# M and N kept unsplit and split on the chip, feed-forward weights split in their ring

## The chip, the cores and the metric

The kernel runs on one core of one Trainium2 chip. The metric is the device time of one execution in microseconds (us). The five engines are named as the profile names them: PE (TensorE, matrix products; PEld is its weight load), DVE (VectorE), ACT (ScalarE), POOL (GpSimd) and SP (SyncE, which here does nothing but issue DMAs, in the order of its program).

## The reference

Two attention layers in float32 over x of 4 batches x 1024 rows x 512:

```
layer 0: q = x wq + bq, k = ctx wk + bk, v = ctx wv + bv      (16 heads of 64, ctx is 64 rows per batch)
         x = LN(softmax(q k'/8 + 2 fside) v wo + bo + x)
layer 1: x = attn(LN1 x, LN1 x) + x      self-attention, 16 heads of 32; q, k, v and weights rounded to 8 bits
         x = attn(LN2 x, ctx) + x        cross-attention, likewise
         x = ((LN3 x) w1a + b1a) * gelu((LN3 x) w1g + b1g) w2 + b2 + x     feed-forward, 512 -> 2048 -> 512
```

The rounding steps need products of nearly float32 precision. So each float32 operand of such a product is split into a high part (float32 rounded to the PE's fp32r format) and a low part (what is left, value minus high), and one product is three matmuls (`three`): high*high, high*low, low*high.

## The kernel before

**Setup.** Layer 0's score matrix is x (wq k'), and its output is p (v wo). Since ctx has only 64 rows per batch, the kernel first multiplies the weights together: for each batch b a matrix M (512 x 1024: all heads' wq k') and a matrix N (1024 x 512: v wo). They are made in groups of four PSUM banks: `GROUPS` has 8 groups of M (4 for each half) and 8 of N. For each group ACT rounds the banks into a staging buffer `st_hi` (`high_rows_M` L998, `high_rows_N` L1009), DVE subtracts into `st_lo` (L1252), and SP stores both to HBM (`kept`): two DMAs for a group of M (L541), eight for one of N (L553). There are two staging buffers of each kind, so ACT waits before a group until the group two earlier has been stored. The raw weights come in through `raw0/raw1` and are split by ACT (L978) and POOL (L816). The setup ends when SP has waited for all stores (its first DMA after it is that of `crow`, L656).

**Chunks.** x is worked in 8 chunks of 512 rows, two for each batch. For a batch: `cross(n)` for its two chunks (layer 0, then q1, k1, v1 of layer 1), then `self_attention(n)` and `middle(n)` (cross-attention, LN3) for each. In `cross` eight steps i compute scores: half 0 (i 0 to 3) with block M0, half 1 with M1; each goes PE -> DVE (add the bias `fbias`, row maximum, subtract) -> ACT (exp) -> DVE (sum) -> POOL (scale, L860) -> PE (transpose, L1808) -> ACT/DVE (split) -> PE (product with N0 or N1). Scores of all steps share PSUM bank 0, so PE's next scores wait until DVE has read the last. POOL adds `crow` to each `fbias` (L853) before DVE can use it.

**Weight blocks.** M0, N0, M1, N1, q1, k1, v1, o1, q2, o2 are 512 x 512 blocks, each loaded by SP as two DMAs, high and low (`load_block`, L604, L605), into one of three slots. A slot is loaded when the block that was in it has been used.

**Feed-forward.** Its 12 groups of steps (`F_ORDER`) use 24 pieces of weights, loaded (`load_piece`, L616, L617) into a ring of 3 pieces. The steps of chunk n are spread as a guest over the slots of later stages (`feed`): for an even chunk over the self-attention and the middle of the next chunk, for an odd one over the next batch's cross, self-attention and middle, for the last one alone. Plans (`host_quarters`) say how many quarter steps are due in each slot; `steps_due` with a lag in slots says when ACT (lag 2) and POOL (lag 3) do their part.

**Prep.** The blocks o1, q2, o2 and the feed-forward weights (15 pieces of work, list `PREP`) aren't split in the setup but during batch 0, through one buffer: SP loads `prep_raw` (L669), ACT rounds (`prep_high`, L1068), POOL subtracts (`prep_low`, L823), SP stores both parts (`keep_prep`, L676, L682). Four are in cross(0), four in cross(1), seven in self_attention(0). SP waits for a store's source and for the buffer between its other DMAs; behind the last of cross(1) it issues the DMA that turns the queries (`turn_queries`, L738), which self_attention(0) needs.

The order on every engine is fixed by the program: each engine has one list of instructions, and waits in it hold all that stands behind.

## Time and profile before

| | |
|---|---|
| time, median of 3 runs | 3646.42 us (3646.25 to 3647.31) |
| the profiled execution | 3642.84 us, its span 3641.0 us |
| PE busy in the span | 2990.9 us (82%) |
| DVE, ACT, POOL busy | 2200.3, 1625.9, 1329.3 us (60%, 45%, 37%) |
| granted PE clock, mean | 0.895 of full speed |
| DMA | 518.20 MB, mean 142 GB/s |

Busy shares are means over stages that differ much. The span begins with the setup (to 224.75 us), then batch 0 (its two crosses to about 527 us, its self-attentions and middles to about 1107 us), then three batches of about 795 us each. In the page's picture of 40 slices of 91 us PE is busy 4, 4, 3, 7, 5, 5, 5 tenths in the first seven slices and 7 to 9 tenths in all but one of those behind them. In a timeline row the first number is the start and the second the time to the end of the row's last instruction, both in us; "[a <-X]" is how long the engine sat idle before it, and what ended that.

### The profile page before, as it was taken

How to read it: one execution, taken by the hardware profiler on the slowest of the kernel's cores; microseconds unless marked ns; L12 is line 12 of the kernel's file. 1: busy time of each engine (PE TensorE's matmuls, PEld its weight loads, DVE VectorE, ACT ScalarE, POOL GpSimd, SP SyncE). 2: the span in 40 equal slices, each digit the busy share in tenths (PEclk: the TensorE clock that was granted, in tenths of full speed). 3: DMA queues.
4: the chain of work that ended last, by engine and by line, in shares of the span. 5: the costliest groups of instructions: out<-in, count | busy, mean ns of one | idle time of the engine just before them, and what ended most of it. 6: DMA issues, size and time to landing. Idle time of an engine off the chain costs nothing.

```text
span 3641.0 us, 50850 instructions
## 1 busy us (share of the span) xinstructions
PE 2990.9 (82%) x19712; PEld 2172.7 (60%) x19712; DVE 2200.3 (60%) x3575; ACT 1625.9 (45%) x2666; POOL 1329.3 (37%) x1025
## 2 busy tenths in 40 slices
PE   4437555769988988989989988889988898899999
PEld 3336442445667765656667755666767655665777
DVE  2335347858756459668656559678465569578431
ACT  3322125637632237547532248457323258367221
POOL 2141315625433215445432225345241335344221
PEclk8668775579999999989999999989999999999999
DMA  6884634322345431332344521332444421332334
GB/s 199 298 286 154 235 123 168 128 110 82 121 151 219 139 148 47 140 122 82 151 153 170 197 84 71 133 116 82 166 165 165 170 79 67 123 116 82 150 129 171
DMA packets 228975, 518.20 MB, mean 142 GB/s; under 512 B 96769, under 2 KB 113409, under 8 KB 206721
## 3 DMA queue, kind: packets, MB, share of 16 engines
q1 hardware_dynamic: 216320, 513.33, 38.9%
q10 hardware_dynamic: 12416, 1.62, 0.3%
q8 instruction: 158, 2.59, 0.3%
q14 instruction: 81, 0.66, 0.1%
HBM read 428.39 MB, written 82.31 MB: 140 GB/s over the span
## 4 chain that ended last, share of the span: by engine, by line
PE 53%; DVE 22%; ACT 7%; issue 5%; POOL 5%; DMA 5%; SPq 2%; ACTq 1%; POOLq 0%; DVEq 0%
PE psum L1587 16%; PE psum L1588 14%; PE psum L1589 14%; DVE mx L1467 8%; DVE w1T L1486 4%; PE psum L1869 3%; DVE den L1473 2%; PE psum L1857 2%; ACT e L1162 2%; ACT psum L1075 1%; SPq L553 1%; DMA kept<-st_lo 1%; ACT ht_hi L1074 1%; PE psum L1883 1%; DVE gate L1378 1%
## 5 line engine op out<-in xcount | busy, mean ns | idle before, releaser
L881 POOL TENSOR_SCALAR w1b<-e,rec 128x1024 f16<-128x1024 f32 x512 | 573.1, 1119 | 717.9 <-DVE rec L1475 501.1
L1467 DVE TENSOR_REDUCE mx<-psum 128x1 f32<-128x1024 f32 x512 | 621.9, 1215 | 74.8 <-PE psum L1858 74.8
L1162 ACT ACTIVATE e<-psum,nb,scale 128x1024 f32<-128x1024 f32 x512 | 617.5, 1206 | 16.8
L1587 PE MATMUL psum<-h_hi,fw_hi 128*128 128x512 f32 x1024 | 465.8, 455 | 16.4 <-DVE h_lo L1252 9.0
L1588 PE MATMUL psum<-h_lo,fw_hi 128*128 128x512 f32 x1024 | 418.0, 408 | 0.0
L1589 PE MATMUL psum<-h_hi,fw_lo 128*128 128x512 f32 x1024 | 417.5, 408 | 0.0
L1869 PE MATMUL psum<-ident,w1b 128*128 128x128 f16 x4096 | 351.3, 235 | 79.8 <-DVE w1T L1486 76.5
L1869 PEld LDWEIGHTS psum<-ident,w1b 128*128 128x128 f16 x4096 | 260.3, 105 | 248.4 <-issue 212.1
L1486 DVE TENSOR_SCALAR w1T<-psum 128x1024 bf16<-128x1024 f16 x512 | 348.6, 681 | 97.5 <-PE psum L1869 92.3
L1587 PE MATMUL psum<-w_hi,ht_hi 128*128 128x512 f32 x640 | 265.9, 415 | 60.7 <-DVE e L1404 32.5
L1341 DVE TENSOR_TENSOR x<-psum,x 128x512 f32<-128x512 f32 x224 | 152.2, 684 | 260.3 <-PE psum L1589 259.9
L1587 PEld LDWEIGHTS psum<-h_hi,fw_hi 128*128 128x128 f32 x1024 | 200.4, 196 | 136.1 <-issue 101.0
L829 POOL TENSOR_TENSOR rstd<-ve,mhalf 128x1 f32<-128x1 f32 x128 | 87.0, 680 | 515.3 <-DVE ve L1349 515.3
L1156 ACT ACTIVATE nb<-mx,nscale 128x1 f32<-128x1 f32 x512 | 149.9, 293 | 278.0 <-DVE mx L1467 270.1
L1588 PE MATMUL psum<-w_lo,ht_hi 128*128 128x512 f32 x640 | 258.8, 404 | 0.0
L1589 PE MATMUL psum<-w_hi,ht_lo 128*128 128x512 f32 x640 | 257.8, 403 | 0.0
L1587 PE MATMUL psum<-fw_hi,u_hi 128*128 128x512 f32 x512 | 226.4, 442 | 22.0 <-POOL u_lo L890 10.4
L890 POOL TENSOR_TENSOR u_lo<-gate,u_hi 128x512 fp32r<-128x512 f32 x128 | 164.0, 1284 | 213.8 <-ACT u_hi L1096 207.8
L1589 PEld LDWEIGHTS psum<-h_hi,fw_lo 128*128 128x128 f32 x1024 | 202.0, 197 | 47.3
L1858 PE MATMUL psum<-k_odd,q_turned 32*128 32x512 bf16 x512 | 220.1, 431 | 0.0
L1588 PEld LDWEIGHTS psum<-h_lo,fw_hi 128*128 128x128 f32 x1024 | 203.2, 198 | 25.9
L1019 ACT ACTIVATE qt<-psum,rounder,inv 128x512 f32<-128x512 f32 x128 | 99.9, 780 | 254.9 <-PE psum L1589 254.9
(175 smaller groups left out, 5904.1 us busy)
## 6 DMA issues: line engine op xcount, KB each, us to landing
fw_hi<-pieces SPq DMA_DIRECT2D x192, 512.0 KB, 3.3
fw_lo<-pieces SPq DMA_DIRECT2D x192, 512.0 KB, 4.3
w_hi<-kept SPq DMA_DIRECT2D x80, 1024.0 KB, 5.0
w_lo<-kept SPq DMA_DIRECT2D x80, 1024.0 KB, 7.7
fbias<-in_fside_Bx16xSxS SPq DMA_DIRECT2D x64, 256.0 KB, 3.5
prep_raw<-in_L_xattn_ff_w SPq DMA_DIRECT2D x12, 1024.0 KB, 8.0
pieces<-prep_hi SPq DMA_DIRECT2D x24, 512.0 KB, 3.5
pieces<-prep_lo SPq DMA_DIRECT2D x24, 512.0 KB, 5.5
```

Of the source, the lines that this page charges most:

```text
L881: pool.tensor_scalar(w1b[u % NH][:], e1[u % NE][:], rec1[:, u % 8:u % 8 + 1], HALF, ALU.mult, ALU.add).then_inc(w1_ready.sem, 1)
L890: pool.tensor_tensor(u_lo[:, m, :], gate[:, m, :], u_hi[:, m, :].bitcast(F32), ALU.subtract).then_inc(u_lo_done.sem, 1)
L1156: act.activation(nb1[:, s % 4:s % 4 + 1], mx1[:, s % 4:s % 4 + 1], ACT.Copy, scale=nscale[:, 0:1]).then_inc(nb_ready.sem, 1)
L1162: act.activation(e1[s % NE][:], psum[:, i:i + 2, :].rearrange("p i n -> p (i n)"), ACT.Exp, bias=nb1[:, s % 4:s % 4 + 1], scale=scale[:, 0:1],
L1341: return emptied_bank(dve.tensor_tensor(xt, bank(bank_of(key)), xt, ALU.add), key)
L1467: dve.tensor_reduce(mx1[:, s % 4:s % 4 + 1], psum[:, i:i + 2, :].rearrange("p i n -> p (i n)"), AX, ALU.max).then_inc(maxed1.sem, 1)
L1486: emptied_bank(dve.tensor_scalar(w1T[u % 8][:].rearrange("p k q -> p (k q)"), bank(bank_of(key)).bitcast(FP16), -HALF, W_HIGH, ALU.add, AL ...
L1587: pe.matmul(o, s_hi, m_hi, start=first, stop=False)
L1588: pe.matmul(o, s_hi, m_lo, start=False, stop=False)
L1589: return pe.matmul(o, s_lo, m_hi, start=False, stop=last)
L1858: ins = pe.matmul(bank(i + 1), q1_turned[turned, hg, t * P:t * P + P], k1[1][turned, hg, :], start=True, stop=True)
L1869: ins = pe.transpose(bank(bank_of(key)).bitcast(FP16)[:, k * P:k * P + P], w1b[u % NH][:, k * P:k * P + P], ident16[:])
```

## The change

M and N are copied from PSUM once, unsplit, half of the banks by ACT and half by DVE, into one of four staging buffers (`st0` to `st3`, in the room of the four of before), and stored once: one DMA for a group of M, four for one of N, into `mixed`. A block M0, N0, M1 or N1 is loaded by one DMA into `w_mixed` (the room of its low part), rounded by ACT (`block_high`, 128 x 2048) and subtracted by POOL (`block_low`, four instructions of 128 x 512) at fixed places: M0 and N0 of the batch's second chunk between its two crosses, M0 of the next batch at the end of the middle before it, the others inside the loop over i. PE waits for the low parts instead of the DMA.

`PREP` keeps only o1, q2 (cross(0)) and o2 (cross(1)). The feed-forward pieces of chunk 0 are loaded from the kernel's inputs into the ring (`unsplit`, in the room of the low part), rounded by ACT (`piece_high`, 128 x 1024) and subtracted by POOL (`piece_low`) in place, and stored from there (`keep_piece`) for the other seven chunks. A piece's place in the ring is loaded again only after that store. The first three are done in middle(0), the other 21 in the slots of chunk 0's feed, ACT with a lag of 2 slots, POOL 3, SP's store 4 (1 each in a middle).

```diff
-LAG_HIGH, LAG_LOW = 2, 3
+LAG_HIGH, LAG_LOW, LAG_KEEP = 2, 3, 4
 def steps_due(plan, lag, i):
     def ended(i):
-        last = max(j - (lag if j in plan.late else 1) for j in range(i - 3, i + 1))
+        last = max(j - (lag if j in plan.late else 1) for j in range(i - lag, i + 1))
         last = min(last, len(plan.ends) - 1)
         return plan.ends[last] // 4 if last >= 0 else 0
     return range(ended(i - 1), ended(i))
+def pieces_due(plan, lag, i):
+    return [v + F_RING for k in steps_due(plan, lag, i) for v in range(PIECES - F_RING) if PIECE_END[v] == k]
...
+PREP = ["o1", "q2", "o2"]
+PREP_IN = {0: ["o1", "q2"], 1: ["o2"]}
...
-GROUP_DMAS = {"M": 2, "N": 8}
+GROUP_DMAS = {"M": 1, "N": 4}
+STAGED = 4
...
             def store_rows_M(half, j):
-                g = GROUPS.index(("M", half, j))
+                g = GROUPS.index(("M", half, j)) % STAGED
+                wait_emptied(sp, ("M", half, j, 1, 0))
                 wait_emptied(sp, ("M", half, j, 1, 1))
-                for part, st in enumerate((st_hi, st_lo)):
-                    sp.dma_start(kept[B * half:B * half + B, part, :, 512 * j:512 * j + 512].rearrange("b p n -> p b n"),
-                                 st[g % 2][:].bitcast(F32)).then_inc(group_stored[g % 2], 16)
+                sp.dma_start(mixed[B * half:B * half + B, :, 512 * j:512 * j + 512].rearrange("b p n -> p b n"), st[g][:]
+                             ).then_inc(group_stored[g], 16)
             def store_rows_N(m):
-                g = GROUPS.index(("N", m))
+                g = GROUPS.index(("N", m)) % STAGED
+                wait_emptied(sp, ("N", m, 1, 0))
                 wait_emptied(sp, ("N", m, 1, 1))
                 r = 8 + B * (m // 4)
-                for part, st in enumerate((st_hi, st_lo)):
-                    for h in range(2):
-                        for odd in range(2):
-                            dst = kept[r:r + B, part, 64 * h:64 * h + 64, 512 * (m % 4):512 * (m % 4) + 512]
-                            sp.dma_start(dst.rearrange("(g o) p n -> o p g n", o=2)[odd],
-                                         st[g % 2][64 * odd:64 * odd + 64, 2 * h:2 * h + 2, :].bitcast(F32)
-                                         ).then_inc(group_stored[g % 2], 16)
+                for h in range(2):
+                    for odd in range(2):
+                        dst = mixed[r:r + B, 64 * h:64 * h + 64, 512 * (m % 4):512 * (m % 4) + 512]
+                        sp.dma_start(dst.rearrange("(g o) p n -> o p g n", o=2)[odd],
+                                     st[g][64 * odd:64 * odd + 64, 2 * h:2 * h + 2, :]).then_inc(group_stored[g], 16)
...
-                sp.dma_start(flat(w_hi[s]), kept[kept_row(key), 0]).then_inc(w_loaded[s], 16)
-                sp.dma_start(flat(w_lo[s]), kept[kept_row(key), 1]).then_inc(w_loaded[s], 16)
+                if name in MIXED:
+                    sp.dma_start(w_mixed[s][:].rearrange("p k n -> p (k n)"), mixed[mixed_row(key)]).then_inc(w_loaded[s], 16)
+                else:
+                    sp.dma_start(flat(w_hi[s]), kept[KEPT[name], 0]).then_inc(w_loaded[s], 16)
+                    sp.dma_start(flat(w_lo[s]), kept[KEPT[name], 1]).then_inc(w_loaded[s], 16)
...
+                if n == 0:
+                    if v >= F_RING:
+                        wait_piece_kept(sp, v - F_RING)
+                    w, row, col = SOURCE[F_ORDER[v // 2]]
+                    if F_ORDER[v // 2][0] == "d":
+                        src = a[w][row + 256 * (v % 2):row + 256 * (v % 2) + 256, :]
+                    else:
+                        src = a[w][:, col + 256 * (v % 2):col + 256 * (v % 2) + 256]
+                    n_cols = src.shape[1]
+                    sp.dma_start(unsplit[r][:].rearrange("p (k n) -> p k n", n=n_cols),
+                                 src.rearrange("(k p) n -> p k n", p=P)).then_inc(raw_piece_loaded[r].sem, 16)
+                    return
                 if r == F_RING:
                     wait_filled(sp, ("a1", n, HG - 1))
-                wait_prep_kept(sp, F_ORDER[v // 2])
+                if n == 1 and v >= PIECES - F_RING:
+                    wait_piece_kept(sp, v)
                 sp.dma_start(fw_hi[r][:].bitcast(F32), pieces[v, 0]).then_inc(f_loaded[r], 16)
                 sp.dma_start(fw_lo[r][:].bitcast(F32), pieces[v, 1]).then_inc(f_loaded[r], 16)
+            def keep_piece(v):
+                r = PIECE_SLOT[0, v]
+                sp.wait_ge(piece_lo_done.sem, piece_lo_done.at(v))
+                sp.dma_start(pieces[v, 0], fw_hi[r][:].bitcast(F32)).then_inc(piece_kept[r].sem, 16)
+                sp.dma_start(pieces[v, 1], fw_lo[r][:].bitcast(F32)).then_inc(piece_kept[r].sem, 16)
             def feed(n, plan, i):
+                if n == 0:
+                    for v in pieces_due(plan, LAG_KEEP, i):
+                        keep_piece(v)
...
-                    load_prep(PREP[4 * n])
+                    load_prep(PREP_IN[n][0])
                 for i in range(3, 7):
                     load_fbias(n, i)
                 load_block((n, "N1"))
-                if n < NC:
-                    keep_prep(PREP[4 * n])
-                    load_prep(PREP[4 * n + 1])
                 load_fbias(n, 7)
                 load_block((n, "q1"))
                 load_block((n, "k1"))
-                if n < NC:
-                    keep_prep(PREP[4 * n + 1])
-                    load_prep(PREP[4 * n + 2])
                 load_block((n, "v1"))
                 if n < NC:
-                    keep_prep(PREP[4 * n + 2])
-                    load_prep(PREP[4 * n + 3])
+                    keep_prep(PREP_IN[n][0])
+                    if n == 0:
+                        load_prep(PREP_IN[n][1])
                 else:
                     for s in range(A_SLOTS):
                         feed(NC * b - 1, FROM_A, A_SLOTS * c + s)
...
+            def block_low(key, ks):
+                s = SLOT[key]
+                pool.wait_ge(block_hi_done.sem, block_hi_done.at(key))
+                for k in ks:
+                    pool.tensor_tensor(w_lo[s][:, k, :], w_mixed[s][:, k, :], w_hi[s][:, k, :].bitcast(F32), ALU.subtract
+                                       ).then_inc(block_lo_done.sem, 1)
...
-                    if n < NC and i == 2:
-                        prep_low(PREP[4 * n])
+                    if i < 2 and n % NC == 0:
+                        block_low((n, "N0"), range(2 * i, 2 * i + 2))
+                    if i in (2, 3):
+                        block_low((n, "M1"), range(2 * (i - 2), 2 * (i - 2) + 2))
+                    if i in (5, 6):
+                        block_low((n, "N1"), range(2 * (i - 5), 2 * (i - 5) + 2))
...
                 if n < NC:
-                    for i in range(1, 4):
-                        prep_low(PREP[4 * n + i])
+                    for name in PREP_IN[n]:
+                        prep_low(name)
+                if n % NC < NC - 1:
+                    block_low((n + 1, "M0"), range(4))
+                    block_low((n + 1, "N0"), range(4))
...
+            def piece_low(v):
+                r = PIECE_SLOT[0, v]
+                pool.wait_ge(piece_hi_done.sem, piece_hi_done.at(v))
+                pool.tensor_tensor(fw_lo[r][:], unsplit[r][:], fw_hi[r][:].bitcast(F32), ALU.subtract
+                                   ).then_inc(piece_lo_done.sem, 1)
             def feed(n, plan, i):
+                if n == 0:
+                    for v in pieces_due(plan, LAG_LOW, i):
+                        piece_low(v)
...
+            def block_high(key):
+                s = SLOT[key]
+                wait_block(act, key)
+                act.activation(w_hi[s][:], w_mixed[s][:], ACT.Copy).then_inc(block_hi_done.sem, 1)
...
+                if n == 0:
+                    block_high((n, "M0"))
+                if n % NC == 0:
+                    block_high((n, "N0"))
                 for i in range(STEPS0 + 2):
+                    if i == 1:
+                        block_high((n, "M1"))
+                    if i == 5:
+                        block_high((n, "N1"))
...
                         quantise((kind, n, m), inv[:, i:i + 1])
-                if n < NC:
-                    prep_high(PREP[4 * n + 2])
-                    prep_high(PREP[4 * n + 3])
+                if n == 0:
+                    prep_high(PREP_IN[n][1])
+                if n % NC < NC - 1:
+                    block_high((n + 1, "M0"))
+                    block_high((n + 1, "N0"))
...
+            def copy_rows_N(m):
+                g = GROUPS.index(("N", m))
+                wait_group_stored(dve, g - STAGED)
+                for pair in range(2):
+                    key = ("N", m, pair, 1)
+                    wait_filled(dve, key)
+                    emptied_bank(dve.tensor_copy(st[g % STAGED][:, 2 + pair, :], bank(bank_of(key))), key)
...
-                            wait_block(pe, (n, f"M{half}"))
+                            pe.wait_ge(block_lo_done.sem, block_lo_done.at((n, f"M{half}", 3)))
```

**SP in the setup, groups of N.** The rows of before stand for four groups of N (of eight), between the loads of two raw weights:

```order
L527 DMA raw1<-in_L1_xattn_a2_wv 128x4x512
L553 DMA kept<-st_hi0 64x2x512 x4
L553 DMA kept<-st_lo0 64x2x512 x4
L553 DMA kept<-st_hi1 64x2x512 x4
L553 DMA kept<-st_lo1 64x2x512 x4
L553 DMA kept<-st_hi0 64x2x512 x4
L553 DMA kept<-st_lo0 64x2x512 x4
L553 DMA kept<-st_hi1 64x2x512 x4
L553 DMA kept<-st_lo1 64x2x512 x4
L527 DMA raw0<-in_L1_xattn_a1_wq 128x4x512
```

The same place in the changed kernel:

```order
L556 DMA raw1<-in_L1_xattn_a2_wv 128x4x512
L582 DMA mixed<-st0 64x2x512 x4
L582 DMA mixed<-st1 64x2x512 x4
L582 DMA mixed<-st2 64x2x512 x4
L582 DMA mixed<-st3 64x2x512 x4
L556 DMA raw0<-in_L1_xattn_a1_wq 128x4x512
```

The 32 stores of these four groups have become 16.

**POOL between the two crosses of a batch** (chunks 2 and 3; `u_lo` is the feed-forward's, the addition of `L0_xattn_bo` and `fbias` belong to chunk 3). Before:

```order
L829 TENSOR_TENSOR rstd<-ve,mhalf 128x1 x8
L890 TENSOR_TENSOR u_lo<-gate,u_hi 128x512 x4
L835 TENSOR_TENSOR x<-x,row_L_xattn_bo 128x2048
L853 TENSOR_TENSOR fbias<-fbias,crow 128x512 x3
L860 TENSOR_TENSOR e_0<-e_0,row_scale 128x512
L853 TENSOR_TENSOR fbias<-fbias,crow 128x512
```

Now:

```order
L879 TENSOR_TENSOR rstd<-ve,mhalf 128x1 x8
L959 TENSOR_TENSOR u_lo<-gate,u_hi 128x512 x4
L873 TENSOR_TENSOR w_lo<-mixed,w_hi 128x512 x8
L885 TENSOR_TENSOR x<-x,row_L_xattn_bo 128x2048
L905 TENSOR_TENSOR fbias<-fbias,crow 128x512 x3
L912 TENSOR_TENSOR e_0<-e_0,row_scale 128x512
L873 TENSOR_TENSOR w_lo<-mixed,w_hi 128x512 x2
L905 TENSOR_TENSOR fbias<-fbias,crow 128x512
L912 TENSOR_TENSOR e_1<-e_1,row_scale 128x512
L873 TENSOR_TENSOR w_lo<-mixed,w_hi 128x512 x2
L905 TENSOR_TENSOR fbias<-fbias,crow 128x512
```

Eight subtractions stand ahead of the addition to x and of the first `fbias`; the other new ones stand between those of the loop.

**SP at the end of cross(1)** (`q_turned` is what self_attention(0) waits for). Before:

```order
L682 DMA pieces<-prep_hi 128x1024 x2
L682 DMA pieces<-prep_lo 128x1024 x2
L669 DMA prep_raw<-in_L_xattn_ff_w 128x4x512
L682 DMA pieces<-prep_hi 512x1x256 x2
L682 DMA pieces<-prep_lo 512x1x256 x2
L738 DMA q_turned<-q_even 64x2048 x2
```

Now:

```order
L635 DMA w_hi<-kept 128x2048
L636 DMA w_lo<-kept 128x2048
L730 DMA kept<-prep_hi 128x2048
L730 DMA kept<-prep_lo 128x2048
L781 DMA q_turned<-q_even 64x2048 x2
```

Behind the load of v1 there stood two prepared pieces of work (each two or more stores, with a load between); now there is one.

## Rows read from the trace of the kernel before

**Rows 1.** Windows of the setup (engines' busy us and counts, PEclk, DMA share, GB/s)

```profile
62.00:92.00 30.00, 14.37 (x128) 13.84 (x127) 9.61 (x16) 10.58 (x23) 4.30 (x1) 0.65 0.92 334
92.00:128.00 36.00, 19.66 (x176) 17.41 (x176) 12.84 (x21) 16.90 (x32) 9.07 (x2) 0.76 0.74 267
128.00:195.00 67.00, 28.53 (x133) 20.85 (x132) 25.89 (x34) 23.24 (x37) 11.19 (x3) 0.58 0.91 308
```

**Rows 2.** Instructions by line and shape, staging: busy us, mean ns | idle before

```profile
L1009 ACT ACTIVATE st_hi<-psum 128x512 fp32r<-128x512 f32 x32 | 16.5, 602 | 41.6 <-DMA kept<-st_lo 41.6
L998 ACT ACTIVATE st_hi<-psum 128x512 fp32r<-128x512 f32 x32 | 16.4, 640 | 33.5 <-DMA kept<-st_lo 33.5
```

**Rows 3.** Timeline of SP, setup: first and last store of N, end

```profile
134.42 3.21 SPq L553 DMA_DIRECT2D kept<-st_hi  x4
...
191.56 3.73 SPq L553 DMA_DIRECT2D kept<-st_lo  x4
...
224.75 0.32 SPq L656 DMA_DIRECT2D crow<-crows  x1
```

**Rows 4.** Timeline of PE, batch 0, where it waited

```profile
251.39 0.50 PE L1587 MATMUL psum<-w_hi,ht_hi 128*128 128x512 f32 x1 [0.85 <-DVE e L1404]
...
299.56 0.66 PE L1808 MATMUL psum<-ident,e 128*128 128x128 f32 x4 [1.14 <-POOL e L860]
...
391.70 0.79 PE L1587 MATMUL psum<-w_hi,ht_hi 128*128 128x512 f32 x1 [19.86 <-DMA w_lo<-kept]
...
410.18 0.79 PE L1587 MATMUL psum<-w_hi,ht_hi 128*128 128x512 f32 x1 [13.00 <-DVE e L1404]
...
457.05 0.66 PE L1808 MATMUL psum<-ident,e 128*128 128x128 f32 x4 [1.14 <-POOL e L860]
...
560.83 0.58 PE L1857 MATMUL psum<-k_even,q_even 32*128 32x512 bf16 x1 [34.15 <-issue]
```

**Rows 5.** Timeline of SP at the end of cross(1)

```profile
554.62 2.33 SPq L738 DMA_DIRECT2D q_turned<-q_even  x2
```

**Rows 6.** Timeline of PE, chunk 3: second scores and last transpose

```profile
1237.01 0.80 PE L1587 MATMUL psum<-w_hi,ht_hi 128*128 128x512 f32 x1 [2.59 <-DVE e L1404]
...
1278.10 0.66 PE L1808 MATMUL psum<-ident,e 128*128 128x128 f32 x4 [1.16 <-POOL e L860]
```

**Rows 7.** Timeline of POOL in self_attention(0), with and without a prep

```profile
657.14 4.50 POOL L823 TENSOR_TENSOR prep_lo<-prep_raw,prep_hi 128x2048 fp32r<-128x2048 f32 x1
...
677.59 4.50 POOL L823 TENSOR_TENSOR prep_lo<-prep_raw,prep_hi 128x2048 fp32r<-128x2048 f32 x1
...
704.44 1.12 POOL L881 TENSOR_SCALAR w1b<-e,rec 128x1024 f16<-128x1024 f32 x1 [0.59 <-issue]
...
721.46 1.12 POOL L881 TENSOR_SCALAR w1b<-e,rec 128x1024 f16<-128x1024 f32 x1 [0.59 <-issue]
```

**Rows 8.** Instructions by line and shape, the two halves of a split

```profile
L823 POOL TENSOR_TENSOR prep_lo<-prep_raw,prep_hi 128x2048 fp32r<-128x2048 f32 x15 | 67.6, 4506 | 111.6 <-ACT prep_hi L1068 111.1
...
L1068 ACT ACTIVATE prep_hi<-prep_raw 128x2048 fp32r<-128x2048 f32 x15 | 28.5, 1903 | 32.9 <-DMA prep_raw<-in_L_xattn_ff_w 30.2 <-DMA prep_raw<-in_L_xattn_a_wo 2.6
```

**Rows 9.** Timeline of POOL, start of chunk 2 and of chunk 3

```profile
1108.81 4.63 POOL L835 TENSOR_TENSOR x<-x,row_L_xattn_bo 128x2048 f32<-128x2048 f32 x1 [7.12 <-PE psum L1791]
...
1229.02 4.63 POOL L835 TENSOR_TENSOR x<-x,row_L_xattn_bo 128x2048 f32<-128x2048 f32 x1 [29.83 <-PE psum L1791]
1234.97 3.72 POOL L853 TENSOR_TENSOR fbias<-fbias,crow 128x512 f32<-128x512 f32 x3 [1.32 <-DMA fbias<-in_fside_Bx16xSxS]
```

**Rows 10.** Timeline of DVE, end of cross(0): normalise of tiles 2 and 3

```profile
322.10 0.54 DVE L1360 TENSOR_SCALAR z<-x,mv,rstd 128x512 f32<-128x512 f32 x1
...
326.41 4.71 DVE L1360 TENSOR_SCALAR z<-x,mv,rstd 128x512 f32<-128x512 f32 x1 [0.66 <-POOL rstd L829]
```

**Rows 11.** Timeline of POOL in self_attention(1), a long instruction among short ones

```profile
837.35 4.55 POOL L835 TENSOR_TENSOR x<-x,row_L_xattn_a_bo 128x2048 f32<-128x2048 f32 x1
```

**Rows 12.** Timeline of PE behind it

```profile
842.86 0.61 PE L1869 MATMUL psum<-ident,w1b 128*128 128x128 f16 x8 [2.65 <-DVE w1T L1486]
```

More of the change, by code:

```diff
@@ L765, in middle @@
                         load_piece(n, 0)
+                    if n == 0 and s == 8:
+                        for v in range(F_RING):
+                            keep_piece(v)
                     if s == 4:
@@ L914, in middle @@
                     host(s)
+                    if n == 0 and s == NT + 2:
+                        for v in range(F_RING):
+                            piece_low(v)
                     if s < NT:
@@ L939, in middle @@
                     host(s)
+                if n % NC == NC - 1 and n + 1 < CHUNKS:
+                    block_low((n + 1, "M0"), range(4))
                 pool.wait_ge(z_ready.sem, z_ready.at((3, n, NT - 1)))
@@ L1184, in middle @@
                     host(s)
+                    if n == 0 and s == NT + 1:
+                        for v in range(F_RING):
+                            piece_high(v)
                 for m in range(HG):
@@ L1200, in middle @@
                     host(s)
+                if n % NC == NC - 1 and n + 1 < CHUNKS:
+                    block_high((n + 1, "M0"))
                 if n >= 1:
```

167 lines of the change are left out of this document (83 added, 84 removed).

## The prediction

> **What bounds the kernel now.** I read the span by stages first: the page's 40 slices, then windows. Behind batch 0 PE is close to its peak, so a gain must be sought where it is not: the setup (to 224.75 us [rows 3]) and batch 0. In the setup's windows PE works 14 of 30, 20 of 36 and 29 of 67 us at a granted clock of 0.58 to 0.76, while the DMA engines are busy 0.92, 0.74 and 0.91 of the time [rows 1]. The lines say the same from the waiting side: ACT sat idle 41.6 + 33.5 = 75.1 us before its 64 staging copies, for the store of a low part [rows 2]. So the setup is bound by 32 MB of M and N going out. The 64 stores of N are issued from 134.42 to 195.3 us [rows 3], 0.95 us for each, 256 KB in each.
>
> Next the timeline of PE through batch 0, reading only the waits in brackets. Three are long: 19.86 us at 391.70 for a weight block, 13.00 us at 410.18 for DVE (which waited for POOL, and that for a `fbias` issued late), 34.15 us at 560.83 before self_attention(0) [rows 4]. All three have one cause. SP issues in order, and a store or load of the prep waits for POOL, which gets to it only at the end of a cross. Behind it on SP stand the next blocks, the next `fbias`, and the turned queries, which went out at 554.62, 6 us before self_attention(0) [rows 5]. Last, POOL's timeline in self_attention(0): with a prep, eight units take 677.59 - 657.14 = 20.45 us; without, 721.46 - 704.44 = 17.02 us [rows 7].
>
> **The change part by part**, against the profiled execution (3642.84 us, of which the span is 3641.0; 3.6 us, or 0.1%, under the median of the runs, 3646.42). A copy of 128 x 2048 on ACT is 1.90 us, the subtraction on POOL 4.51 us [rows 8]; I take a fourth of the latter, 1.13 us, for one of 128 x 512, and 0.95 and 2.25 us for a piece of 128 x 1024.
>
> *Setup, -54 us.* Half the bytes and 32 + 8 instead of 64 + 16 stores. For N, 32 x 0.95 = 30 us go. In M the waits of 33.5 us [rows 2] go in part: four buffers take half 0 of M without any wait, but behind it PE needs the split of wv and wo, and stores of 1 MB remain. I take 24 of the 33.5. The tail from 195.3 to 224.75 us (three more weights split and stored one after another) stays, as it has its own chain. DVE and ACT copy half of the banks each, side by side: less work than before. Bounds: 30 us, if only N's stores count, and 75 us, all of ACT's waits. I take 54, near the middle, since every wait in rows 2 is for a store.
>
> *cross(0), -3 us.* From its second scores to its last transpose 299.56 - 251.39 = 48.2 us [rows 4]; chunk 3, with no prep in it, needs 1278.10 - 1237.01 = 41.1 us [rows 6]. Of these 7 us the prep at i = 2 goes, but M0's split now stands between the load and PE's first matmul: 1.9 + 4.5 us, less the second megabyte that isn't loaded. Net -3, between -7 and +4.
>
> *cross(1), -22 us.* The waits of 19.86 and 13.00 us lose their cause. What comes in: at the end of cross(0) ACT still does q2's prep (1.9), then M0 and N0 (3.8), POOL q2 (4.5), M0 and N0 (9.0), the addition to x (4.6) and one `fbias` (1.3). Counted from the last rounding of v1 at about 370 us, the first `fbias` is ready at 370 + 1.9 + 4.5 + 9.0 + 4.6 + 1.3 = 391 us, and PE's second scores start at 393 us instead of 410.18: -17. The prep within the loop goes as well: 457.05 - 410.18 = 46.9 us [rows 4] against chunk 3's 41.1: -5. Bounds -10 and -30.
>
> *Start of self_attention(0), -32 us.* Only o2's store is still ahead of the turned queries, and POOL has made it before the q and k products end. So they are turned before v1 is done, and of the 34.15 us about 2 remain, for rounding v1. Bounds -28 and -34.
>
> *self_attention(0), -23 us.* Seven preps go, at 20.45 - 17.02 = 3.4 us each [rows 7]: -24, I take -23. If DVE then bound less than I think, -30; if the last preps were hidden, -18.
>
> *Chunk 0's feed, +15 us.* 24 x (0.95 on ACT + 2.25 on POOL). Three pieces are done in middle(0), beside products and LN: +1. The other 21 lie in self_attention(1) and middle(1). A 4.55 us addition among POOL's short instructions there [rows 11] left PE waiting 2.65 us for DVE [rows 12]. So I count the two pairs of pieces that come due together in self_attention(1) at 2.6 us each, its ten single ones at 0.5, and middle(1), where ACT and POOL wait in their order for a DMA just issued and `e`'s exp and scaling stand behind them, at 4: 14. A piece is wanted two steps after its place is free, and the work for it takes a slot or two less, so PE should seldom wait for it. Bounds 0 and 38 us (21 + 3 pieces at 2.65 x 2.25/4.55 = 1.3, and 7 for the DMA waits).
>
> *Between the two crosses of batches 1 to 3, +27 us.* In chunk 3 POOL starts the addition to x at 1229.02, and `fbias` at 1234.97, 1.32 us late for its DMA [rows 9]. PE's second scores start at 1237.01 [rows 6]. Now POOL first waits for ACT's split of M0 (1.9 us behind the last v1, about 1227.3), then subtracts 9.0: 1238.2. Addition to 1242.8, first `fbias` 1244.1, one DVE read, PE at 1244.9: +7.9. With two subtractions each in i = 2 and 3, and PE's clock lower behind a longer wait (its matmul there took 0.80 us, in rows 6, where others take 0.39 to 0.50): +9. Three times. There is no cover: PE's guest steps in a cross are one ahead of the loop and the rest behind it. Bounds 0 and 15 each.
>
> *Start of chunks 2, 4 and 6, +9 us.* POOL waited 7.12 us before the addition at 1108.81 [rows 9]; M0's subtraction, 4.5 us, lies there. N0's four and M1's four stand in i = 0 to 3, where POOL's `fbias` and scaling come 1 to 2 us later than PE wants them. +3 each, bounds 0 and 7. N1's, at i = 5 and 6, lie in POOL's gaps of over 3 us.
>
> *DVE and POOL at once.* One normalise took 4.71 us where its like takes 0.54, exactly while POOL subtracted 128 x 2048 [rows 10]. That one stays (prep o1 and o2 are at the same place). The new subtractions are four short ones, so I count 1 us for a collision, within the terms above. The Trainium skill (SBUF — State Buffer, "Who interferes with whom") says that the two engines share a pair of ports and that whichever comes second is blocked for the whole instruction of the first. By that rule the trace agrees, the time per collision goes down with the instruction (1.1 us instead of 4.5), and the sum stays; it speaks against the change only by their number.
>
> Sum: -54 - 3 - 22 - 32 - 23 = -134; +15 + 27 + 9 = +51; net -83. 3642.84 - 83 = 3560, and at the median's level 3563. I say 3562 us.
>
> **Rivals.**
> 1. *The setup gives little.* Its bytes halve, but stores of 64 partitions are slow, raw weights and their splits stand in the same queues, and PE is at half clock. For: the window of 92 to 128 us has only 0.74 of DMA [rows 1], so something else ends waits there. Against: rows 2. -30 instead of -54: 3586 us.
> 2. *The added work shows fully in crosses and feed*, at the upper bounds: 38 + 45 + 21 = 104 instead of 51: 3615 us. This includes DVE blocked by POOL often. For: each engine's list is fixed, and the loop over i has little slack in i = 0 to 3. Against: POOL is idle between its instructions in most of the loop.
> 3. *It hides fully.* 3562 - 45 = 3517 us. For: PE bound in most slots. Against: nothing else covers POOL's nine us between crosses.
> 4. *Slower: POOL and ACT become the bound.* 32 blocks x (1.90 + 4.51) = 205 us and 24 pieces x 3.2 = 77 us, all of it in lists where PE's next operand stands behind. That is 282 us for 134 gained: 3642.84 - 134 + 282 = 3791 us at the worst, and slower than before from 134 of 282 exposed, 48%. Rows 9's 7.12 us and 29.83 us of waiting POOL speak against: at most block starts it has that room. I count 18% as exposed.
>
> **How the numbers follow.** Forecast 0.66; rival 1 0.13; rival 2 0.12; rival 3 0.06; rival 4 0.03. The forecast's own bounds, added as if independent (setup +24/-21, feed +24/-15, chunk starts +22/-30, batch 0 +15/-15), give about +44/-43; I cut both ends somewhat and take 3530 to 3608, which reaches over rival 1 and most of the way to rival 2. What this kernel's measurement can tell from no change is about 0.2%, 7 us. Faster needs 83 us of margin to vanish: 0.95; within 0.2%: 0.02; slower: 0.03.
>
> **What would show it.** In the profile after: the first `crow` load near 170 us, ACT's waits before the staging copies under 20 us in all; no PE wait over 8 us in cross(1); self_attention(0) beginning 2 to 3 us behind v1; w1b in even steps of 17 us for eight. In chunks 3, 5 and 7 PE's wait before its second scores near 6 to 8 us, with POOL's `w_lo` ahead of it. Stages behind batch 0: about 12 us longer for each batch. Wrong would be: `crow` later than 195 us (rival 1), batches over 25 us longer (rivals 2 and 4), or PE waiting for `fw_lo` in self_attention(1) by more than 15 us.

## The result and the profile after

The changed kernel takes 3561.86 us (median of 4 runs, 3559.77 to 3564.55), the kernel before 3646.34 us beside it: a ratio of 0.9774, 95% interval 0.976 to 0.9788. Forecast were 3562 us and 0.977. The profiled execution took 3564.55 us, with a span of 3562.7 us against 3641.0 us before. The terms below are differences of these two traces and add up to their 78.3 us; the medians differ by 84.5 us.

Each stage is measured from one instruction to the same instruction of the next stage, so that nothing is counted twice: the `crow` load on SP, the first and the last reciprocal `row_scale` of each cross on DVE, the first and the last `mx` of self_attention.

| stage | forecast, us | measured, us |
|---|---|---|
| setup, to `crow` | -54 | -63.7 |
| cross(0), from `crow` to its last `row_scale` | -3 | -1.9 |
| cross(1) | -22 | -21.4 |
| start of self_attention(0) | -32 | -33.1 |
| self_attention(0) | -23 | -24.2 |
| middle(0), self_attention(1), middle(1), to chunk 2 | +15 | +24.4 |
| chunks 2 to 7, between the crosses and in the odd chunks' loops | +27 | +29.2 |
| chunks 2 to 7, the rest | +9 | +12.4 |
| sum | -83 | -78.3 |

The stages don't cut quite as the forecast did. The start of chunk 2, with M0's split, lies in the sixth row as measured, while the forecast had it in the last, as a part of 3 us.

The setup after, in windows (PE, PEld, DVE, ACT, POOL busy, PEclk, DMA share, GB/s):

```profile
62.00:92.00 30.00, 27.57 (x292) 26.84 (x292) 13.02 (x20) 20.80 (x39) 12.14 (x4) 0.87 0.83 290
92.00:128.00 36.00, 23.45 (x147) 18.68 (x144) 15.79 (x20) 15.97 (x22) 11.80 (x4) 0.81 1.03 375
128.00:161.00 33.00, 6.25 (x21) 4.70 (x19) 5.81 (x6) 5.38 (x4) 12.88 (x3) 0.60 0.88 331
```

Against [rows 1] PE works 27.57 of the first 30 us instead of 14.37, at a granted clock of 0.87 instead of 0.65. It no longer waits there for a staging buffer: with two buffers again (experiment 6) the same window has 18.60 us at 0.74. In the next window the DMA share is 1.03, after 0.74 before: the DMA engines have something to do all the time, and the stores set the pace of N. The waits before ACT's 32 staging copies (busy, mean ns | idle before) answer to [rows 2]:

```profile
L1070 ACT ACTIVATE st<-psum 128x512 f32<-128x512 f32 x16 | 9.2, 614 | 2.7 <-PE psum L1742 2.2
L1080 ACT ACTIVATE st<-psum 128x512 f32<-128x512 f32 x16 | 8.7, 594 | 17.6 <-DMA mixed<-st 17.6
```

2.7 + 17.6 = 20.3 us instead of 75.1, at the edge of the forecast's "under 20". (Before, ACT made 64 copies; now it makes 32, and DVE the others.) What is left of the waits lies in N. SP's rows, with the first and the last stores of N and the end of the setup, answer to [rows 3]:

```profile
99.85 15.80 SPq L582 DMA_DIRECT2D mixed<-st  x16
...
124.66 6.81 SPq L582 DMA_DIRECT2D mixed<-st  x8
...
161.05 0.32 SPq L711 DMA_DIRECT2D crow<-crows  x1
```

M now ends 134.42 - 99.85 = 34.6 us earlier. N takes 131.47 - 99.85 = 31.6 us instead of 60.9, and the tail behind it 29.6 us as before.

PE's timeline through batch 0, where it waited, answers to [rows 4]:

```profile
185.42 0.80 PE L1685 MATMUL psum<-w_hi,ht_hi 128*128 128x512 f32 x1 [10.58 <-POOL w_lo L873]
...
315.42 0.80 PE L1685 MATMUL psum<-w_hi,ht_hi 128*128 128x512 f32 x1 [9.76 <-POOL w_lo L873]
...
326.77 0.80 PE L1685 MATMUL psum<-w_hi,ht_hi 128*128 128x512 f32 x1 [6.66 <-DVE e L1502]
...
441.00 0.39 PE L1955 MATMUL psum<-k_even,q_even 32*128 32x512 bf16 x1 [1.66 <-DVE v L1388]
```

The wait of 34.15 us is down to 1.66. In cross(1) 9.76 and 6.66 us stand in the places of 19.86 and 13.00. Before the first scores PE now waits for M0's split: 10.58 us in cross(0), where it waited 6.10 us for the load before, and 9.76 us in cross(1). There POOL subtracts q2's prep first, and M0 behind it:

```profile
305.95 4.52 POOL L865 TENSOR_TENSOR prep_lo<-prep_raw,prep_hi 128x2048 fp32r<-128x2048 f32 x1 [40.67 <-ACT prep_hi L1139]
310.44 9.88 POOL L873 TENSOR_TENSOR w_lo<-mixed,w_hi 128x512 fp32r<-128x512 f32 x8
```

In chunks 3, 5 and 7, with no prep, the same wait is 2.60 us. That of 9.76 us I had not foreseen (no wait over 8 us was forecast there), though it lies within the stage's sum. The turned queries are issued 126 us earlier than in [rows 5], 12.5 us before PE wants them:

```profile
428.49 1.16 SPq L781 DMA_DIRECT2D q_turned<-q_even  x2
```

POOL in self_attention(0) makes eight units in 518.32 - 501.10 = 17.22 us, evenly, as the prediction said for the stretch without a prep [rows 7]:

```profile
501.10 1.12 POOL L940 TENSOR_SCALAR w1b<-e,rec 128x1024 f16<-128x1024 f32 x1 [0.59 <-issue]
...
518.32 1.12 POOL L940 TENSOR_SCALAR w1b<-e,rec 128x1024 f16<-128x1024 f32 x1 [0.89 <-issue]
```

Between the crosses, chunk 3, POOL and then PE (to be read against [rows 9] and [rows 6]):

```profile
1110.47 9.95 POOL L873 TENSOR_TENSOR w_lo<-mixed,w_hi 128x512 fp32r<-128x512 f32 x8 [29.71 <-ACT w_hi L1152]
1120.37 4.51 POOL L885 TENSOR_TENSOR x<-x,row_L_xattn_bo 128x2048 f32<-128x2048 f32 x1
1124.82 3.74 POOL L905 TENSOR_TENSOR fbias<-fbias,crow 128x512 f32<-128x512 f32 x3
```

```profile
1126.87 0.80 PE L1685 MATMUL psum<-w_hi,ht_hi 128*128 128x512 f32 x1 [8.32 <-DVE e L1502]
```

Eight subtractions take 9.95 us, the addition to x follows, then `fbias`, and PE waits 8.32 us where it waited 2.59. The same wait is 6.66, 8.32 and 6.72 us in chunks 1, 5 and 7. The forecast was 6 to 8 us, and two lie a little above.

The long normalise of [rows 10] is still there, beside `prep_lo` of o1. The subtraction that runs beside it on POOL, and DVE:

```profile
260.78 4.50 POOL L865 TENSOR_TENSOR prep_lo<-prep_raw,prep_hi 128x2048 fp32r<-128x2048 f32 x1
```

```profile
260.85 4.71 DVE L1458 TENSOR_SCALAR z<-x,mv,rstd 128x512 f32<-128x512 f32 x1 [0.66 <-POOL rstd L879]
...
1127.57 1.53 DVE L1509 TENSOR_TENSOR e<-e,row_max 128x512 f32<-128x512 f32 x1
...
1133.53 0.69 DVE L1509 TENSOR_TENSOR e<-e,row_max 128x512 f32<-128x512 f32 x1
```

The last two rows are one DVE operation in two steps of chunk 3. It took 1.53 us while POOL ran the short `fbias` additions (1124.82 to 1128.56), and 0.69 us without them: 0.84 us for one collision with a short instruction, near the 1 us that the prediction took for it. This collision isn't new, the kernel before has it at the same place:

```profile
1237.71 1.53 DVE L1411 TENSOR_TENSOR e<-e,row_max 128x512 f32<-128x512 f32 x1
```

Where DVE's operation begins first, the new subtraction is the one that grows. At 1137.40 it again took 0.69 us, and the subtraction that began 0.08 us behind it took 1.77 us instead of the median 1.29.

### The profile page after: what moved, and what is told of

Read it like the earlier page. It is cut to its first block, busy times and chain, and to the rows that moved or that the text cites. A ratio compares the mean times of both kernels' runs of the same rounds, so it can differ in the third digit from the quotient of the medians.

```text
span 3562.7 us, 50726 instructions
## 1 busy us (share of the span) xinstructions
PE 2979.5 (84%) x19712; PEld 2166.1 (61%) x19712; DVE 2193.1 (62%) x3543; ACT 1670.1 (47%) x2678; POOL 1506.3 (42%) x1165
## 3 DMA queue, kind: packets, MB, share of 16 engines
q8 instruction: 158, 2.59, 0.3%
## 4 chain that ended last, share of the span: by engine, by line
PE 52%; DVE 22%; POOL 9%; ACT 8%; issue 5%; DMA 3%; SPq 1%; ACTq 1%; POOLq 0%; DVEq 0%
PE psum L1685 15%; PE psum L1686 14%; PE psum L1687 14%; DVE mx L1565 8%; DVE w1T L1584 4%; PE psum L1967 3%; POOL w_lo L873 3%; ACT e L1256 2%; PE psum L1955 2%; DVE den L1571 2%; POOL x L885 1%; ACT psum L1146 1%; PE psum L1981 1%; DMA fw_lo<-pieces 1%; ACT ht_hi L1145 1%
## 5 line engine op out<-in xcount | busy, mean ns | idle before, releaser
L1349 DVE TENSOR_TENSOR ht_lo<-psum,ht_hi 128x512 fp32r<-128x512 f32 x160 | 108.5, 689 | 186.3 <-ACT psum L1146 132.3
L873 POOL TENSOR_TENSOR w_lo<-mixed,w_hi 128x512 fp32r<-128x512 f32 x128 | 169.4, 1349 | 123.0 <-ACT w_hi L1152 123.0
```

Of the source, the lines that this page charges most:

```text
L873: pool.tensor_tensor(w_lo[s][:, k, :], w_mixed[s][:, k, :], w_hi[s][:, k, :].bitcast(F32), ALU.subtract).then_inc(block_lo_done.sem, 1)
```

## The experiments

Ten kernels ran, each beside the kernel before. Where an expectation names a part, the edit is relative to the changed kernel unless it says otherwise. "Trace" means the difference of the two profiled executions at the same instruction.

**1. The ring alone.** The kernel before with the feed-forward part of the change; M and N are stored and loaded split.

```diff
-            sp.dma_start(w_mixed[s][...], mixed[mixed_row(key)])
+            sp.dma_start(flat(w_hi[s]), kept[kept_row(key), 0])
+            sp.dma_start(flat(w_lo[s]), kept[kept_row(key), 1])
```

> The kernel before with one part of the change alone: the feed-forward weights are split piece by piece in the ring; M and N are stored split as before (setup, crosses and block loads unchanged). Theory A (the terms of the prediction are separate, and those of batch 0 belong to the prep that goes): the setup ends at 224 to 225 us as before, cross(0) ends 7 us earlier, cross(1) 20 us, self_attention(0) starts another 30 us earlier and runs 24 us shorter, the pieces cost 24 us in self_attention(1) and middle(1), batches 1 to 3 as before: 3646 - 7 - 20 - 30 - 24 + 24 = 3589 us (3580 to 3597). Rival B (the gain in batch 0 needs also the shorter block loads, since SP stays late with w_hi and w_lo): the waits before self_attention(0) and in cross(1) go in half, 3615 us or more.

Measured: 3573.89 us, ratio 0.9805 (0.979 to 0.982). SP's `crow`, then PE's second scores of cross(1) and of chunk 3:

```profile
226.42 0.32 SPq L702 DMA_DIRECT2D crow<-crows  x1
```

```profile
380.70 0.80 PE L1636 MATMUL psum<-w_hi,ht_hi 128*128 128x512 f32 x1 [10.93 <-DVE e L1453]
...
1167.43 0.80 PE L1636 MATMUL psum<-w_hi,ht_hi 128*128 128x512 f32 x1 [2.63 <-DVE e L1453]
```

Rival B is refuted: the waits before self_attention(0) go wholly (-33.1 us in the trace) though the block loads still move two parts. Theory A holds in its places but missed by 15 us in size. Cross(1) gained 28.6 us, not 20. POOL does not have M0's and N0's subtractions at the end of cross(0) here; in the whole change they eat a part of the gain (experiment 3 gets 6.1 us of it back in cross(1)). The pieces cost +22.4 us. The setup and each stretch from one cross to the next in batches 1 to 3 stay within 2 us of before; PE waits 2.63 us in chunk 3, as before.

**2. M and N alone.** The kernel before with the other part; the twelve preps of the feed-forward weights stay.

```diff
-PREP = ["o1", "q2", "o2"]
+PREP = ["o1", "q2", "o2"] + list(F_ORDER)
```

> The kernel before with the other part alone: M and N stored unsplit and split when loaded; the feed-forward weights go through the prep as before. Theory A: setup 64 us shorter, batches 1 to 3 42 us longer, and in batch 0 the waits in cross(1) and before self_attention(0) stay; POOL's 9 us of subtractions at the end of cross(0) come on top of four preps there, +5 to +10: 3646 - 64 + 42 + 7 = 3631 us (3622 to 3640). Rival B (the two parts add up exactly to the whole change of -84.5): 3646 - 84.5 + 57 = 3619 us. Rival C (the store of unsplit rows is not what shortened the setup, but something that the ring changed there): setup under 30 us shorter, over 3650 us.

Measured: 3626.51 us, ratio 0.9949 (0.9934 to 0.9964), inside theory A's range. PE in cross(1), before self_attention(0) and in chunk 3:

```profile
341.22 0.80 PE L1636 MATMUL psum<-w_hi,ht_hi 128*128 128x512 f32 x1 [26.28 <-POOL w_lo L840]
...
506.53 0.58 PE L1906 MATMUL psum<-k_even,q_even 32*128 32x512 bf16 x1 [33.72 <-issue]
...
1195.33 0.79 PE L1636 MATMUL psum<-w_hi,ht_hi 128*128 128x512 f32 x1 [8.29 <-DVE e L1453]
```

The 34 us before self_attention(0) stay, and in cross(1) waits of 26.28 and 5.86 us stand in the places of the former two. So the batch-0 gains belong to the preps that went, and the setup's gain and the 8.3 us between crosses to M and N. By medians the two parts give -71.5 and -18.9, together -90.4; the whole change measured -84.5. In the traces cross(1) gains 25.9 us by the two parts (-28.6 + 2.7) and 21.4 together. But the spans of the same traces give -63.7 and -9.8, together -73.5, against -78.3 for the whole change, so the 6 us by medians are no measure of an interaction: the runs of this kernel alone lie 12 us apart. Rival B's exact sum is 7.5 us under the measured median.

**3. N0 later.** In the odd chunks N0's low part moves into steps 0 and 1 of the loop.

```diff
                     block_low((n + 1, "M0"), range(4))
-                    block_low((n + 1, "N0"), range(4))
...
-                    if i < 2 and n % NC == 0:
+                    if i < 2:
                         block_low((n, "N0"), range(2 * i, 2 * i + 2))
```

> The changed kernel, but in chunks 1, 3, 5 and 7 POOL subtracts only M0 ahead of the addition to x; N0's four subtractions stand in steps 0 and 1 of the loop, as in the even chunks. Theory A (POOL's serial list M0, N0, x, fbias sets PE's wait of 6.7 to 8.3 us before the second scores): 4.5 us earlier at each second score, given back 0 to 2 us in the steps 0 and 1 (e and fbias behind N0's subtractions): 4 x (-3.5) = -14, 3548 us (3543 to 3554). Rival B (the wait is ended by another thing, the fbias load or ACT's w_hi, and POOL only looks late): no change, 3560 to 3563 us. Rival C (N0's low part is then late for PE's first use in step 3): PE waits for w_lo there, slower than 3562.

Measured: 3547.06 us (3546.24 to 3547.45), ratio 0.973 (0.9715 to 0.9744). PE before the second scores of chunk 3:

```profile
1114.41 0.80 PE L1684 MATMUL psum<-w_hi,ht_hi 128*128 128x512 f32 x1 [3.42 <-DVE e L1501]
```

3.42 us instead of 8.32 us. Taking some 5 us of POOL's work from ahead of `fbias` moves PE's wait by 4.9 us and shortens the stretch between the crosses by 4.5 us: POOL's list was the cause, and not ACT or the load. The loop of chunk 3 keeps its length.

**4. The addition to x later.** The same list, another of its entries.

```diff
-                wait_filled(pool, ("xT", n, KT - 1))
-                add_bias(n, "L0_xattn_bo")
...
+                    if i == STEPS0 + 1:
+                        wait_filled(pool, ("xT", n, KT - 1))
+                        add_bias(n, "L0_xattn_bo")
```

> The changed kernel, with the addition of the bias row to x (4.5 us on POOL) moved in all eight crosses from ahead of the first fbias to the last step of the loop, where DVE needs it some 6 us later. Theory A (serial list on POOL): odd chunks -4.5 us each; even chunks 2, 4, 6 -1 to -3 each, since PE's first scores end about when the first fbias is ready; chunk 0 -2; the end of the loop costs 0 to 1 each: -18 - 6 - 2 + 4 = -22, 3540 us (3533 to 3548). Rival B: the addition then blocks DVE or is late for its residual, +2 to +4 us in each cross, and the gain is eaten: 3555 to 3565 us.

Measured: 3543.54 us (3540.75 to 3546.02), ratio 0.9723 (0.9707 to 0.9739). PE in chunk 3, the addition at its new place, and DVE behind it:

```profile
1115.05 0.80 PE L1686 MATMUL psum<-w_hi,ht_hi 128*128 128x512 f32 x1 [2.54 <-DVE e L1503]
```

```profile
1160.12 4.62 POOL L885 TENSOR_TENSOR x<-x,row_L_xattn_bo 128x2048 f32<-128x2048 f32 x1
```

```profile
1164.77 0.69 DVE L1440 TENSOR_TENSOR x<-psum,x 128x512 f32<-128x512 f32 x1 [1.21 <-POOL x L885]
```

PE waits 2.54 us. The loop of chunk 3 keeps its length. Behind it DVE waits 1.21 us for the addition, a little over the 0 to 1 us that A allowed, and the stretch from chunk 2's last `row_scale` to chunk 3's first is 3.6 us shorter. Theory A holds.

**5. Every group stored twice.** Copies and buffers as in the changed kernel, bytes and stores as before.

```diff
-                sp.dma_start(mixed[...], st[g][:]).then_inc(group_stored[g], 16)
+                for to in (mixed, second):
+                    sp.dma_start(to[...], st[g][:]).then_inc(group_stored[g], 16)
```

> The changed kernel, but every staged group of M and N is stored twice, the second time into a tensor that nothing reads: the same copies and four buffers, but 32 MB and 64 + 16 stores as in the kernel before. Theory A (the stores alone set the setup, and half of them is what it gained): N 32 x 0.95 = +30 us, M +25 to +34 us, crow near 220 us: 3562 + 60 = 3622 us (3610 to 3630). Rival B (it was the split: ACT's rounding and DVE's subtraction one behind the other from two buffers): the setup grows by less than 20 us, 3580 us or less. Rival C (N is bound by the number of stores, M by the copies): +30 in N, 0 to 5 in M, 3595 us.

Measured: 3605.18 us, ratio 0.9886 (0.9872 to 0.9901). SP's first and last stores of N and its `crow`, and ACT's waits:

```profile
113.13 4.39 SPq L585 DMA_DIRECT2D mixed<-st  x4
...
169.62 3.89 SPq L585 DMA_DIRECT2D second<-st  x4
...
203.64 0.32 SPq L714 DMA_DIRECT2D crow<-crows  x1
```

```profile
L1073 ACT ACTIVATE st<-psum 128x512 f32<-128x512 f32 x16 | 9.1, 609 | 10.6 <-DMA second<-st 9.4 <-PE psum L1745 0.7
L1083 ACT ACTIVATE st<-psum 128x512 f32<-128x512 f32 x16 | 8.7, 595 | 38.4 <-DMA second<-st 38.4
```

`crow` comes 42.6 us later than in the changed kernel: M 13.3, N (173.51 - 113.13 = 60.4 us) 28.8, tail 0.5. N is what the prediction said, 32 stores of 0.95 us each. Of M's 34.6 us only 13.3 are bytes and stores. The edit doubles both the bytes and the number of stores, so it doesn't tell one from the other. The measured time lies between theory A and rival C.

**6. Two staging buffers.**

```diff
-STAGED = 4
+STAGED = 2
```

> The changed kernel with two staging buffers instead of four. Theory A (ACT's waits in M went because four buffers take half 0 of M without a wait, and because of the fewer bytes in equal parts): M +5 to +15 us, N unchanged (its stores follow at 0.95 us each in either case): 3572 us (3566 to 3578). Rival B (only the bytes count): 3560 to 3564 us. Rival C (with two buffers N's copies and stores alternate as before): 30 us more, 3592 us.

Measured: 3592.2 us, ratio 0.9848 (0.9834 to 0.9863): the number of rival C, but not its place. ACT's waits:

```profile
L1070 ACT ACTIVATE st<-psum 128x512 f32<-128x512 f32 x16 | 8.8, 614 | 27.6 <-DMA mixed<-st 26.4 <-PE psum L1742 1.1
L1080 ACT ACTIVATE st<-psum 128x512 f32<-128x512 f32 x16 | 8.7, 594 | 23.5 <-DMA mixed<-st 23.5
```

M's waits go from 2.7 to 27.6 us, N's from 17.6 to 23.5 us. In the trace M is 19.1 us longer, N 4.1, the tail 2.2. So the two additional buffers are worth more in M than the halved bytes (19.1 against 13.3 us), and together they make 32.4 of its 34.6 us. That sum is argued: no run has two buffers and the doubled stores with the new copies. Theory A had the mechanism and half of its size; rival B is refuted.

**7. Pieces split later in middle(1).**

```diff
-    return [v + F_RING for k in steps_due(plan, lag, i) for v in ...]
+    every = Plan(plan.ends, range(len(plan.ends) + 8))
+    return [v + F_RING for k in steps_due(every, lag, i) for v in ...]
```

> The changed kernel, but in the middle stages of chunk 1 the split of a piece of the feed-forward weights is due 2 slots (ACT), 3 (POOL) and 4 (SP's stores) behind the step that frees its place, as in self_attention, instead of 1 slot for all. Theory A (the 16.5 us that middle(1) lost are ACT waiting in its order for a DMA just issued, the weights' rows landing some 10 us later, with the affine of the layer norm behind it): the wait of 14.55 us before o2/h2's products falls under 4 us, 3550 us (3546 to 3554). Rival B (the piece itself is late for the host's matmuls): PE waits for fw_lo instead and nothing is gained, 3560 to 3564 us. self_attention(1) stays as it is (+7 us) in either case.

First the place in the changed kernel, on SP, ACT, POOL and PE:

```profile
888.21 0.41 SPq L653 DMA_DIRECT2D unsplit<-in_L_xattn_ff_w  x1
```

```profile
897.83 1.06 ACT L1169 ACTIVATE fw_hi<-unsplit 128x1024 fp32r<-128x1024 f32 x1 [13.84 <-DMA unsplit<-in_L_xattn_ff_w]
```

```profile
898.97 2.35 POOL L947 TENSOR_TENSOR fw_lo<-unsplit,fw_hi 128x1024 fp32r<-128x1024 f32 x1 [7.90 <-ACT fw_hi L1169]
```

```profile
901.65 0.77 PE L1685 MATMUL psum<-ht_hi,w_hi 128*128 128x512 f32 x1 [14.55 <-DVE ht_lo L1349]
```

The load of a piece's rows, issued at 888.21, ends ACT's wait at 897.83, 9.6 us later. ACT waits 13.84 us for it, and the layer norm's affine stands behind it, for which PE waits 14.55 us. Measured with the edit: 3556.09 us (3551.39 to 3559.49), ratio 0.975 (0.9736 to 0.9765). ACT, POOL and PE:

```profile
919.42 1.99 ACT L1170 ACTIVATE fw_hi<-unsplit 128x1024 fp32r<-128x1024 f32 x2
```

```profile
931.90 4.66 POOL L948 TENSOR_TENSOR fw_lo<-unsplit,fw_hi 128x1024 fp32r<-128x1024 f32 x2
```

```profile
934.38 0.76 PE L1686 MATMUL psum<-h_hi,fw_hi 128*128 128x512 f32 x1 [9.33 <-POOL fw_lo L948]
```

The 14.55 us are gone, and 9.33 us have come in their place, for `fw_lo`. In the trace 7.2 us are gained from the end of self_attention(1) to chunk 2, and 5.8 us by medians, where A said 12. Neither theory as stated; the wait moved to POOL's order.

**8. The three edits together.**

> The changed kernel with the three edits together: N0's subtractions in the loop, the addition to x at the loop's end, the later split of the pieces. Theory A (POOL's list ahead of the first fbias, M0, N0, x, is one chain, so that both parts count until the 8.8 us between the crosses are used up): -15 - 18 - 10 = -43, 3519 us (3514 to 3526). Rival B (the next thing in line, the fbias load or the second scores' own operands, already stands 5 us behind): each odd chunk gains 5 instead of 8: 3532 us.

Measured: 3525.1 us (3518.98 to 3525.9), ratio 0.9662 (0.9645 to 0.9678), inside theory A's range. Of the single runs' gains, 14.8 + 18.3 + 5.8 = 38.9 us, 36.8 are found together.

**9. The three edits, with POOL one slot earlier.**

```diff
+    def ended(i):
+        last = max(j - (lag if j < S_SLOTS or lag == 2 else lag - 1) for j in range(i - lag, i + 1))
...
+    return [v + F_RING for k in range(ended(i - 1), ended(i)) for v in ...]
```

> N0's subtractions in the loop and the addition to x at the loop's end, as in the run with three edits, but in middle(1) the split of a piece is due 2 slots behind on ACT and also 2 on POOL (3 for SP's stores), where that run had 2, 3 and 4. There PE waited 9.33 us for fw_lo: ACT had rounded two pieces at 919.4 to 921.4, and POOL took them up at 931.9, behind the scaling of e. Theory A (POOL's place in its order made the piece late, not the load): that wait falls to 0 to 3 us, and the kernel is 5 to 9 us under the one with three edits, 3518 us (3514 to 3522). Rival B (the load of the weight rows sets the pace, one piece in some 13 us): PE or ACT waits as long at another place, 3523 to 3528 us.

Measured: 3517.02 us (3515.34 to 3518.57), ratio 0.9654 (0.964 to 0.9669). POOL's two subtractions, formerly at 931.90, and PE's longest wait of that stretch:

```profile
919.89 4.72 POOL L951 TENSOR_TENSOR fw_lo<-unsplit,fw_hi 128x1024 fp32r<-128x1024 f32 x2
```

```profile
915.24 0.86 PE L2039 MATMUL psum<-ident,w2b 128*128 128x128 f16 x8 [4.15 <-POOL w2b L1007]
```

No wait for `fw_lo` is left. Against experiment 10, which has the pieces as in the changed kernel, the stretch from the last `row_scale` of cross(1) to the first of chunk 2 is 14.0 us shorter (616.4 against 630.4 us), and its part behind self_attention(1) 15.1 us: most of middle(1)'s loss was the order of the splits. Theory A holds, and the load is not too slow. This is the fastest of all versions, 1.3% under the changed kernel.

**10. The two edits of experiments 3 and 4.**

> The changed kernel with two edits alone: N0's subtractions in the loop and the addition to x at the loop's end; the pieces are split as in the changed kernel. Theory A (the two are parts of one chain on POOL and add up until the 8.8 us between the crosses are gone): 3562 - 15 - 18 + 2 = 3531 us (3527 to 3535), with PE's wait before the second scores back near 1 to 2.6 us in chunks 3, 5 and 7. Rival B (each hides a part of the other): 3538 us or more.

Measured: 3533.66 us (3532.44 to 3534.84), ratio 0.9701 (0.9685 to 0.9717). PE in chunk 3, first and second scores:

```profile
1109.90 0.79 PE L1685 MATMUL psum<-w_hi,ht_hi 128*128 128x512 f32 x1 [2.59 <-POOL w_lo L873]
...
1115.17 0.50 PE L1685 MATMUL psum<-w_hi,ht_hi 128*128 128x512 f32 x1 [0.86 <-DVE e L1502]
```

The wait before the second scores is 0.86 us, less than before the change. From the last `row_scale` of one cross to the first of the next it takes 90.4 us, 1.3 us more than before the change; what stays is PE's 2.59 us before the first scores, for M0's low part. Of the single runs' gains, 14.8 + 18.3 = 33.1 us, 28.2 are found together, inside theory A's range: the two add up, less some 5 us.

## Why the prediction was right, and where it was off

The time was right to 0.2 us by luck. The mechanisms were in the main those of the forecast, but three terms were off by 5 to 10 us, and nearly cancelled (-9.7 in the setup, +9.4 in the pieces, +5.6 in batches 1 to 3). In the traces the sum is still 4.7 us off; the medians hide that, since the profiled execution of this kernel was the slowest of four, and that of the kernel before lies 3.6 us under its median.

- **Setup, -63.7 for -54.** The step that was mis-sized is M's: "I take 24 of the 33.5". It was 34.6. I counted the halved bytes and took the buffers for a share; experiments 5 and 6 give 13.3 us for bytes and stores and 19.1 us for the buffers. N (29.3 us for 30), and the tail that stays, were right.
- **cross(0), -1.9 for -3.** Both halves were there: +5.4 us up to the first `row_scale` (M0's split), -7.3 us where the prep at i = 2 went.
- **cross(1), -21.4 for -22; start of self_attention(0), -33.1 for -32; self_attention(0), -24.2 for -23.** Experiments 1 and 2 put all three down to the preps, as the prediction did: the ring alone has all three gains, M and N alone has none. What M and N take back in cross(1) depends on what else is late: 2.7 us where the preps keep PE waiting anyway (experiment 2), 28.6 - 21.4 = 7.2 us where POOL's list is all that is left.
- **The pieces, +24.4 for +15.** In the parts: middle(0) +1.0 for +1; self_attention(1) +6.4 for +10; middle(1) with the way to chunk 2 +17.0 for +4. Of the 17.0 some 2 us are M0's split at chunk 2 (M and N alone have +2.0 there, the ring alone +14.3), which the forecast counted elsewhere. The failed step is "middle(1), where ACT and POOL wait in their order for a DMA just issued ... at 4". The mechanism was named and its price was not worked out. The bound of 7 us for it was too low as well. The split is due one slot behind the load's issue, and a slot of middle(1) lasts, by an estimate, 5.6 us (22 slots from self_attention(1)'s last `mx` at 838.1 to SP's next `crow` at 961.2 us), against up to 9.6 us for the landing. Experiments 7 and 9 gain 7.2 and 15.1 us of that stretch by the order alone.
- **Between the crosses, +25.2, and +4.0 in the odd chunks' loops, for +27 together.** POOL's list M0, N0, x, `fbias` was the right chain; experiments 3, 4 and 10 take 4.9, 5.8 and 7.5 us from PE's wait of 8.32 us by taking entries out of it, and 4.5, 3.6 and 7.5 us from the stretch.
- **The rest, +12.4 for +9.** Of it 4.2 us are the even chunks' loops and 8.2 us stretches from one pair of chunks to the next. Of these 2.2 and 2.1 us lie between the last `mx` ahead of chunks 4 and 6 and their first `row_scale`, where M0's subtraction stands; with 1.4 us for each loop that is near the 3 us for each start. The other 3.9 us are not clear of noise: the way from cross(3)'s last `row_scale` to self_attention(2) takes 75.9 us in the changed kernel, and 74.0 and 76.2 us in experiments 5 and 7, which leave it as it is.

Of the rivals, the setup giving little (1) is refuted by `crow` at 161.05. Of the added work 24.4 + 41.6 = 66 us show, where the forecast had 51, the added work hidden (3) 6, and shown fully (2) 104: nearer to the forecast than to either, though 15 us above it. POOL and ACT as the bound (4): 66 of 282 us are 23%, where I had counted 18% and the sign turned at 48%. The collisions of DVE and POOL that were looked at stayed small, as counted. One slip of the prediction is in its range: it says that both ends were cut, but 3608 lies 46 us above 3562, and its own sum gave 44.

## What to carry to other kernels

Work that is moved from the setup into the stages is paid for only where it stands ahead of what PE waits for next. So look at each engine's list in front of that wait and put first what is needed first: here N0's four subtractions cost 4.5 us ahead of chunk 3's `fbias`, and under 0.1 us in its loop (experiment 3). When an engine in the middle of its order waits for a load, give the load its landing time in slots, and count the engine behind it as well. When traffic is halved, ask separately what the bytes gave and what the buffers gave that became free.
